# Attention and expert layer on one core: batch 0's query and key rows are moved to their stacks in two halves, and two pieces of VectorE work stand later

## The reference

```python
q = layernorm(x).reshape(B, T, 16, 16) * scale          # scale = 16 ** -0.25, the same for k
scores = einsum('bthd,bshd->bhts', q, k)                 # k and v are the context, by head
out = einsum('bhts,bshd->bthd', softmax(scores), v).reshape(B, T, 256)
x = x + out @ w_proj.T + b_proj
gate = top2_softmax(layernorm(x) @ Wg.T)                 # 8 experts, 2 of them kept
hidden = silu(z @ W1[e].T) * (z @ W2[e].T)               # z = layernorm(x), hidden size 682
x = x + sum over e of gate[e] * (hidden @ W3[e].T)
```

## Time and profile before

| | |
|---|---|
| median of 3 runs | 897.08 us (895.11 to 900.03) |
| the profiled execution, own time | 896.09 us |
| its span | 894.3 us |
| busy share of the span | PE 88%, DVE 67%, ACT 61%, POOL 52% |
| chain that ended last, by engine | PE 58%, POOL 12%, ACT 7%, SP's queue 7% |
| first score matmul starts | 25.92 us |
| first exponential starts | 48.76 us |
| the nine operations of `split_bias` | 10.62 to 17.02 us, with the memset of 0.17 us first |

### The profile page before, as it was taken

The page is one execution under the profiler, slowest core; times in us unless marked ns, Lnnn a source line. Parts: engine busy times, 40 slices in busy tenths (PEclk is TensorE's granted clock), DMA queues, the critical chain, the costliest instruction groups (busy, mean ns, idle before and its releaser), DMA issues.

```text
span 894.3 us, 19943 instructions
## 1 busy us (share of the span) xinstructions
PE 786.5 (88%) x6344; PEld 476.9 (53%) x6344; DVE 603.1 (67%) x1258; ACT 541.7 (61%) x938; POOL 467.7 (52%) x432
## 2 busy tenths in 40 slices
PE   0478888989989898888989899997999999999995
PEld 0112223323322332232237688886888888888884
DVE  4788988979979799799715557553555555555552
ACT  3258779878878887868773445452444444444442
POOL 4566357787878978787623665222333222222222
PEclk9999999989989999999989999998999999999998
DMA  8584666939378384865283969999996879483832
GB/s 171 139 223 148 207 131 214 198 107 272 120 258 177 134 238 144 226 160 185 91 278 141 240 183 286 286 276 212 265 262 160 203 210 260 76 242 55 245 48 24
DMA packets 109794, 167.51 MB, mean 187 GB/s; under 512 B 58656, under 2 KB 87072, under 8 KB 105120
## 3 DMA queue, kind: packets, MB, share of 16 engines
q1 hardware_dynamic: 96288, 148.77, 59.4%
q0 software_dynamic: 13440, 17.90, 10.6%
HBM read 119.75 MB, written 42.55 MB: 181 GB/s over the span
## 4 chain that ended last, share of the span: by engine, by line
PE 58%; POOL 12%; ACT 7%; SPq 7%; issue 6%; DMA 3%; DVE 2%; POOLq 0%; ACTq 0%; DVEq 0%
PE ps L1376 9%; PE ps L1378 9%; PE ps L1380 9%; PE ps L1304 8%; POOL slots L474 5%; ACT probs L846 5%; PE ps L1394 4%; PE ps L1396 4%; PE ps L1289 4%; PE ps L1398 4%; PE ps L1276 3%; SPq L622 3%; POOL w_lo L763 2%; POOL w_in L752 2%; DVE neg_max L974 1%
## 5 line engine op out<-in xcount | busy, mean ns | idle before, releaser
L974 DVE TENSOR_REDUCE neg_max<-ps 128x2 f16<-128x1024 f32 x256 | 307.5, 1222 | 36.2 <-PE ps L1276 32.7
L846 ACT ACTIVATE probs<-ps 128x1024 f32<-128x1024 f32 x256 | 257.5, 1026 | 80.6 <-PE ps L1289 76.7
L773 POOL DMA_INDIRECT out<-y,aim x72 | 112.6, 1564 | 249.4 <-DVE y L1207 163.7
L1376 PE MATMUL ps<-zt,w 128*128 128x256 f16 x792 | 217.8, 275 | 7.2 <-DMA w<-w_parts 5.8
L1378 PE MATMUL ps<-zt,w 128*128 128x256 f16 x792 | 217.7, 275 | 0.0
L1380 PE MATMUL ps<-zt,w 128*128 128x256 f16 x792 | 217.6, 275 | 0.0
L875 ACT ACTIVATE silu<-ps 128x256 f32<-128x256 f32 x216 | 82.5, 382 | 193.1 <-PE ps L1380 189.2
L1188 DVE SCALAR_TENSOR_TENSOR hid<-ps,silu 128x256 f32<-128x256 f32 x216 | 91.8, 425 | 143.4 <-ACT silu L875 139.8
L1276 PE MATMUL ps<-k_stack,q_stack 48*128 48x512 f16 x512 | 105.5, 410 | 50.4 <-ACT probs L846 31.7
L1304 PE MATMUL ps<-probs,v_ext 128*32 128x512 f32 x1024 | 139.9, 618 | 4.7 <-ACT heads L909 3.7
L1289 PE MATMUL ps<-q_stack,k_stack 49*128 49x512 f16 x512 | 102.0, 397 | 12.8 <-DVE neg_max L974 6.4
(11 more groups left out here) (126 smaller groups left out, 963.8 us busy)
## 6 DMA issues: line engine op xcount, KB each, us to landing
w<-w_parts SPq DMA_DIRECT2D x36, 1408.0 KB
w<-w_parts SPq DMA_DIRECT2D x36, 768.0 KB
w_in<-in_w SPq DMA_DIRECT2D x16, 704.0 KB
v_ext<-in_v SPq DMA_DIRECT2D x8, 1024.0 KB, 6.4
k_stack<-k SPq DMA_DIRECT2D x48, 128.0 KB, 6.8
q_stack<-qt SPq DMA_DIRECT2D x48, 128.0 KB, 7.9
w_in<-in_w SPq DMA_DIRECT2D x8, 768.0 KB
w_parts<-w_hi SPq DMA_DIRECT2D x16, 352.0 KB, 2.6
```

Of the source, the lines that this page charges most:

```text
L773: nc.gpsimd.indirect_dma_start(out=out, out_offset=bass.IndirectOffsetOnAxis(ap=aim[frm][:, t, 0:1].bitcast(U32), axis=0), in_=y[frm][:, t ...
L846: nc.scalar.activation(probs[g % 2][:, j:j + 2, k, :], pair_banks[PLACE["exp", u] % 3], ACT.Exp, scale=0.25).then_inc(s_exp, 1)
L974: nc.vector.tensor_reduce(neg_max[b % 2][:, g, c:c + 9:8], pair_banks[PLACE["max", u] % 3], AX.X, ALU.max, negate=True).then_inc(s_red, 1)
L1376: nc.tensor.matmul(dst, w[:, kk, 1, cols], z16[:, kk, :], start=(kk == 0), stop=False)
```

## The change

Batch 0's twelve copies to the stacks become twenty-four, each of which takes 64 partitions of its source (one half of the heads, `first_part`) instead of 128. The first half of the heads comes first and has semaphores of its own, `s_kfirst` and `s_qfirst`. PE waits for these before its first scores, and for the second half only in slot 8. The host lays out batch 0's queries and keys so that the two halves of the heads lie on the two halves of the partitions. The load of batch 1's `x_in` moves between the halves. DVE takes batch 1's statistics in quarter slots 4, 6, 8, 10 and 12, that is in slots 1 to 3 and between the maxima, instead of ahead of slot 0. `split_bias` moves from slot -10 to slot 10.

```diff
+AT_BIAS = 10
+SECOND_PREP = 4
...
+            def first_part(stack, part, j, half, done):
+
+                some = slice(half * PAIRS // 2, (half + 1) * PAIRS // 2)
+                for par in range(2):
+                    row = 64 * par + j * D
+                    sp.dma_start(stack[row:row + D, some, :], part[half * HALF:(half + 1) * HALF, par, :]
+                                 ).then_inc(done, 16)
...
             sp.wait_ge(s_kh, 1)
-            k_part(0, 0, 0)
-            k_part(0, 2, 0)
+            first_part(k_stack[0], k16[0], 0, 0, s_kfirst)
+            first_part(k_stack[0], k16[0], 2, 0, s_kfirst)
             sp.wait_ge(s_kl, 1)
-            k_part(0, 1, 1)
+            first_part(k_stack[0], k16[1], 1, 0, s_kfirst)
             sp.wait_ge(s_mr, misc_use(0, "turn_q", 0) + 1)
-            q_part(0, 0, 0)
-            q_part(0, 1, 0)
+            first_part(q_stack[0], qt16[0], 0, 0, s_qfirst)
+            first_part(q_stack[0], qt16[0], 1, 0, s_qfirst)
             sp.wait_ge(s_mr, misc_use(0, "turn_q", 1) + 1)
-            q_part(0, 2, 1)
+            first_part(q_stack[0], qt16[1], 2, 0, s_qfirst)
+            sp.wait_ge(s_ql, 1)
+            sp.dma_start(x_in[:, :, :], xq_l[1]).then_inc(s_xin, 16)
+            for j, part in enumerate((0, 1, 0)):
+                first_part(k_stack[0], k16[part], j, 1, s_kd)
+            for j, part in enumerate((0, 0, 1)):
+                first_part(q_stack[0], qt16[part], j, 1, s_qd)
...
                 for n, off in enumerate(STEP_PREP):
                     for b in due(q, off, 4):
-                        prep_step(b, n)
+                        if b != 1:
+                            prep_step(b, n)
+                    if q == SECOND_PREP + 2 * n:
+                        prep_step(1, n)
...
-                    dve.wait_ge(s_cst, 5)
+                if slot == AT_BIAS:
                     split_bias()
...
-                    if s == 0 and half == 0:
+                    if b == 0 and s == 0 and half == 0:
+                        pe.wait_ge(s_kfirst, 96)
+                        pe.wait_ge(s_qfirst, 96)
+                    if s == (0 if b else H // 2) and half == 0:
                         pe.wait_ge(s_kd, (b + 1) * 96)
                         pe.wait_ge(s_qd, (b + 1) * 96)
```

More of the change, by code:

```diff
@@ L411, in build @@
         s_qd, s_kd = sem("s_qd"), sem("s_kd")
+        s_qfirst, s_kfirst = sem("s_qfirst"), sem("s_kfirst")
         s_mrow = [sem(f"s_mrow{g}") for g in range(4)]
@@ L590, in _ @@
                 for b in due(slot, AT_X_IN):
-                    if b >= 1:
+                    if b >= 2:
                         sp.wait_ge(s_ql, b)
@@ L864, in misc @@
                         ge(act, s_qd, b * 96)
+                        if b == 1:
+                            act.wait_ge(s_qfirst, 96)
                         nc.scalar.copy(qt16[i][:, :, :].rearrange("p a t -> p (a t)"), misc16).then_inc(s_mr, 1)
@@ L912, in _ @@
                     ge(act, s_kd, b * 96)
+                    if b == 1:
+                        act.wait_ge(s_kfirst, 96)
                     nc.scalar.copy(k16[0][:, :, :], kt_in[:, :, :]).then_inc(s_kh, 1)
@@ L1324, in misc @@
                     if name == "project":
+                        if b == 0 and i == 0:
+                            pe.wait_ge(s_bias, K_BIAS)
                         nc.tensor.matmul(misc_bank[:, 0:W], ones16[:, :], bias16[:, :], start=True, stop=False)
@@ L1411, in _ @@
                     pe.wait_ge(s_small, 48)
-                    pe.wait_ge(s_bias, K_BIAS)
                     pe.wait_ge(s_zero, 4)
@@ L1437 @@
     c = np.asarray(ctx_1024)
-    x_q = np.asarray(x).reshape(B, T, PAIRS, 2, D).transpose(0, 1, 3, 4, 2)
-    k_t = c.reshape(B, T, PAIRS, 2, D).transpose(0, 4, 2, 3, 1).reshape(B, P, 2, T)
+    x_q = np.asarray(x).reshape(B, T, 2, PAIRS // 2, 2, D)
+    x_q = np.concatenate([x_q[:1].transpose(0, 1, 4, 2, 5, 3).reshape(1, T, W),
+                          x_q[1:].transpose(0, 1, 4, 5, 2, 3).reshape(B - 1, T, W)])
+    k_t = c.reshape(B, T, 2, PAIRS // 2, 2, D)
+    k_t = np.concatenate([k_t[:1].transpose(0, 2, 5, 3, 4, 1).reshape(1, P, 2, T),
+                          k_t[1:].transpose(0, 5, 2, 3, 4, 1).reshape(B - 1, P, 2, T)])
     v = np.zeros((B, P, NT, H, 32), np.float32)
```

## The result

| | before | changed |
|---|---|---|
| median of 20 runs each, on the same chip | 900.14 us (892.81 to 909.61) | 903.82 us (896.31 to 908.02) |
| ratio, changed to before | | 1.0056, 95% interval 1.0036 to 1.0077 |
| a second set of runs: median, ratio | 897.52 us (23 runs) | 903.84 us (12 runs), 1.0052 (1.0020 to 1.0084) |
| profiled execution, own time and span | 896.09 and 894.3 us | 903.62 and 901.8 us |

The changed kernel is slower by about 5 us, 0.5 to 0.6% by the ratios; the medians differ by 3.7 us in the first set and 6.3 us in the second. The ratios leave out slow runs (over 1.5% above the fastest of the same kernel: two of the kernel before in the first set, one in the second), so they are not quotients of these medians. Each set of runs compares with runs of the kernel before on the same chip, so ratios are to be compared, not medians across sets.

The account below looks back on a forecast made before the run. The prediction took completion of batch 1's `mv`, through POOL's weight split and SP's queue, to set the exponentials' start. Terms 3.5 + 1.9 = +5.4 us gave 901.5 us (902.5 on the median), range 898.5 to 907.5 us.

Parts of the forecast that it names:

- The chain: Before batch 0's exponentials: 19.13 us from batch 1's `mv` through POOL and SP to PE's second scores, untouched by the change.
- The first term: Start of batch 0: `mv` complete at 32.4 us instead of 28.98, behind seven maxima; +3.5 us on the second scores.
- The landing: Last first-half copy to `q_stack`: issued at 19.0 us, lands about 3.0 us later, so PE starts at 22.0 us.
- The pile: Batch 0's stack copies: whole ones pile up; half-size ones drain in 0.55 us, under their 0.60 us issue, so none.
- the second rival: Batch 0's stack copies: half-size ones take as long as whole ones, `mv` 7.3 us late, 906.3 us; chance 0.13.
- The second term: Bias's split in slot 10: costs 2.8 us, third group's maxima 2.2 us later, slot 16 starts +1.9 us later.
- Rival 1: Smaller slip: copies land fast (+2.8 us), loop absorbs most of the bias (0 to 1.5 us); 900 to 901.4 us; chance 0.26.
- Rival 3: Start of batch 0: the sixteen maxima bind, not the way through `mv`; 894.6 us, or 892.7 with bias hidden; chance 0.09.

Follow-up runs that it names:

- the bias alone: The kernel before with only the bias's split moved to slot 10; ratio to the kernel before 1.0028 (0.9993 to 1.0064).
- halves alone: The changed kernel with batch 1's statistics and the bias's split back where the kernel before had them; ratio 0.9949, in a second set 0.9985.

## Why the prediction was right

**The chain.** The step on which the forecast rests, that `mv` of batch 1 sets the start of the exponentials through POOL's weight split and SP's queue, is shown three times: it moved with the statistics by 6.1 us one way and 7.3 us the other, and it was cut by moving SP's first write of weights. The signs that the prediction named are there, each 1.3 to 1.8 us ahead of its time: PE's first scores at 20.68 us (forecast 22), `mv` complete at 30.94 us (32.4), the first write at 39.71 us (41.2), the first copy of maxima at 42.58 us (44), the second scores at 49.79 us (51.6). Of this, 0.8 us is that the changed kernel's execution began its copies earlier.

**The first term, +3.5 us, measured +2.8 us.** The order was right (seven maxima and four statistics ahead of `mv`: 9.6 us from the first maximum, 9.77 forecast). The landing was estimated too long. Counted from the first copy, the last one was issued 0.1 us earlier than forecast, it landed 0.4 us sooner, and `mv` took 0.16 us less behind the first maximum; together that is the 0.7 us between 3.5 and 2.8. Transfers to `q_stack` in the changed kernel, 8 to 20 us:

```profile
L523 SPq DMA_DIRECT2D q_stack<-qt x6: 547/594/595, 15.0 to 18.1; - x6
...
DMA to landing us min/median/max: 2.4/2.6/2.6
```

It was 2.6 us against the 3.0 us that I took. One reading was wrong without consequence: the last copy to `q_stack` at 19.0 us did not wait for the turned queries. ACT had finished these at 18.10 us, and the six copies are issued at SP's pace, one in 0.6 us, from 15.82 us on. The pile is gone, as worked out, and the second rival (half-size copies that take as long as whole ones) is wrong. So is what the prediction made of the Trainium skill (SBUF — State Buffer, "Door 1: The DMA port swizzle"), by which 64 source partitions have the rate of 32: a drain as slow as that of whole copies would have piled up again, and all six landed in 2.4 to 2.6 us. No run changed the number of partitions at equal bytes, so the rule itself is not tested.

**The second term, +1.9 us, measured +2.4 us at an earlier place.** It is measured at the third transposition, in both profiles of the changed kernel and with the bias alone, where the forecast had 2.2 us. The operations cost the 2.8 us that were worked out, slot 10 was free of POOL as said, and slack took back 0.4 us rather than 0.65. That a further 0.3 us would be absorbed in slot 16 could not be seen, as the clock's spread is larger there; the changed kernel shows no wait for the maxima's row in slot 16.

**Sum.** 2.8 + 2.4 = 5.2 us, against 5.4 forecast; the ratios say 5.0 and 4.7 us on 900 us. That the sum is closer than its terms is luck: the first was 0.7 us too large and the second 0.5 us too small. Rival 1 had two halves. The first, that the copies land fast and cost +2.8 us, is what was measured; the second, that the loop absorbs the bias down to 0 to 1.5 us, is out by the fixed 2.4 us. Rival 3 (the gain arrives) failed at the condition that was named for it: `mv` before 28.98 us. With halves alone that condition holds (25.47 us), and a gain does arrive, but through `mv` and not through the sixteen maxima, as the rival had it. That kernel's interval lay below 1 in one set of runs (0.9949) and reached 1.0017 in the second (0.9985). The second scores are 3.0 us earlier on the mean of its two profiles; a gain in the whole time is shown in one set of two.

**What the prediction lacked.** It took the pace of slots 12 to 15 as fixed. They took 12.8 us before and 14.5 us in the changed kernel's first profile, as TensorE stayed at its lower clock for longer, and two profiles of the same kernel can differ by 2.6 us there. I took this at first for part of the bias's price, and had expected 4 us in all for the bias in two experiments; the repeated profiles show the same spread without the bias in slot 10, so that reading is not supported. Slot 16, forecast for 77.8 us, began near 78 us with this in it, so its agreement shows less than it seems to.

## What to carry to other kernels

An engine that starts earlier gains nothing until the wait that ends last is shown to depend on it. Here a small operation for the next batch stood behind the work that was brought forward, and another engine's queue stood behind that operation; work that looks like filler should be followed to everyone who is queued behind it before it is moved. The queue that issues transfers is an engine of its own: in this kernel it has hardly a gap for some 30 us, and of each place that was won ahead of it a part or all was given back further down the queue. And small VectorE copies on SBUF belong where VectorE waits anyway, or at least where GpSimd is idle: the same nine operations cost nothing ahead of slot 0, where they took 6.4 us beside GpSimd but VectorE had to wait for a load, 2.4 us in slot 10, and some 14 us in slot 20 (the ratios 1.0183 against 1.0024, the fallen clock included).

## What was not expected of the hardware

- Copies of 128 KB to 16 partitions pile up: 3.5 to 5.6 us for the k copies to land and 6.6 to 6.8 us for the last q copies. The six first-half copies of 64 KB to `q_stack`, issued at the same pace, all landed in 2.4 to 2.6 us.
- TensorE's pairs of matmuls fell to their short duration at times 8 us apart in two executions of one kernel, with the same instructions (62.96 and 70.72 us). The clock fell again behind a wait of 1.98 us in one execution of halves alone, where one of 0.85 us in another left it; with the bias in slot 20 it fell within the wait of 9.98 us (granted clock 1.00 from 91 to 92 us, 0.50 from 93 us on). Whether the length of the wait decided between the first two is not settled, since there is one of each.
- Four short VectorE operations (0.21 to 0.42 us alone) took 1.33 to 2.82 us each beside GpSimd.
